# Causal masks from TensorE to VectorE, wider transposes, and a picking matrix made later, in an attention and mixture-of-experts block

## What is computed

```python
h = layernorm(x) * (1 + ca) + sa
q, k, v = (split_heads(h @ W + b) for W, b in ...)     # 16 heads of width 8
att = softmax(where(causal, q @ k.T / sqrt(8), -inf))
y = (att @ v) @ Wo + bo
x = x + ga * (layernorm(y) * gamma + beta)
h = layernorm(x) * (1 + cb) + sb
x = x + gb * (shared_ffn(h) + sum over the top 2 of 8 experts of coef * expert_ffn(h))
```

## Time and profile before

| | |
|---|---|
| runs | 516.39, 521.52, 522.48 us; median 521.52 us |
| span of the profiled execution | 517.1 us, 9099 instructions; the page gives no time of its own beside the span |
| TensorE busy | 468.1 us (91%), 3122 matmuls |
| VectorE busy | 374.1 us (72%), 1046 instructions |
| ScalarE busy | 272.8 us (53%) |
| GpSimd busy | 252.8 us (49%) |
| mean granted TensorE clock | 0.960 |

### The profile page before, as it was taken

The page is one execution under the profiler, slowest core; times in us unless marked ns, Lnnn a source line. Parts: engine busy times, 40 slices in busy tenths (PEclk is TensorE's granted clock), DMA queues, the critical chain, the costliest instruction groups (busy, mean ns, idle before and its releaser), DMA issues. The chain is left out here.

```text
span 517.1 us, 9099 instructions
## 1 busy us (share of the span) xinstructions
PE 468.1 (91%) x3122; PEld 239.6 (46%) x3122; DVE 374.1 (72%) x1046; ACT 272.8 (53%) x571; POOL 252.8 (49%) x344
## 2 busy tenths in 40 slices
PE   3478889999999999999999999999999998899897
PEld 2224334544644553545454453545454454344554
DVE  4687746997589748985699648985789757875165
ACT  2214554775558535765568435764567534755321
POOL 7534356533865077535764077525763251523530
PEclk9857996999999999999999999999999999999999
DMA  4674452332333234323443134323433222003000
GB/s 106 164 171 115 117 152 50 85 94 85 106 99 87 56 113 117 100 69 106 114 101 90 42 111 112 97 61 104 129 83 98 83 77 60 2 2 104 1 21 22
DMA packets 40942, 45.31 MB, mean 88 GB/s; under 512 B 9448, under 2 KB 32520, under 8 KB 40896
## 3 DMA queue, kind: packets, MB, share of 16 engines
q1 hardware_dynamic: 35652, 40.92, 29.9%
q10 hardware_dynamic: 5244, 3.82, 2.6%
HBM read 33.70 MB, written 10.61 MB: 86 GB/s over the span
## 5 line engine op out<-in xcount | busy, mean ns | idle before, releaser
L799 ACT ACTIVATE probs<-s_bank 128x512 f32<-128x512 f32 x320 | 179.9, 596 | 97.2 <-PE s_bank L1199 95.6
L979 DVE CUSTOM_DVE_ANT_0 s_bank<-s_bank,causal_row 128x512 f32<-128x512 f32 (+1 forms) x256 | 156.2, 642 | 28.9 <-PE s_bank L1179 27.3
L1179 PE MATMUL s_bank<-k_stack,q_stack 72*128 72x256 bf16 (+3 forms) x512 | 129.6, 314 | 10.7 <-DVE row_max L979 5.1
L1199 PE MATMUL s_bank<-q_stack,k_stack 75*128 75x128 bf16 (+3 forms) x512 | 120.4, 308 | 15.3 <-DMA q_stack<-max_rows 7.6
L662 POOL TENSOR_SCALAR_AFFINE_SELECT probs<-probs 128x512 f32<-128x512 f32 (+1 forms) x96 | 75.5, 794 | 116.2 <-ACT probs L799 116.0
L1199 PEld LDWEIGHTS s_bank<-q_stack,k_stack 75*128 75x128 bf16 x512 | 43.1, 100 | 92.0 <-ACT probs L799 41.1
L1218 PE MATMUL pv_bank<-probs,v_aug 128*32 128x512 f32 (+3 forms) x1024 | 83.2, 444 | 0.0
L1179 PEld LDWEIGHTS s_bank<-k_stack,q_stack 72*128 72x128 bf16 x512 | 47.3, 100 | 75.0 <-DVE row_max L979 38.5
L984 DVE TENSOR_REDUCE row_max<-s_bank 128x2 f32<-128x512 f32 (+1 forms) x96 | 64.5, 687 | 16.9 <-PE s_bank L1183 16.0
L1218 PEld LDWEIGHTS pv_bank<-probs,v_aug 128*32 128x32 f32 x1024 | 26.1, 110 | 43.8 <-issue 34.2
L1067 DVE SCALAR_TENSOR_TENSOR silu_sb<-tanh_sb,gate_bank 128x512 f32<-128x512 f32 x38 | 26.1, 687 | 21.6 <-ACT tanh_sb L852 21.3
(11 more groups left out here) (183 smaller groups left out, 546.0 us busy)
## 6 DMA issues: line engine op xcount, KB each, us to landing
k_stack<-k_scr SPq DMA_DIRECT2D x96, 96.0 KB
q_stack<-q_scr SPq DMA_DIRECT2D x93, 96.0 KB
coef_all<-coef_scr SPq DMA_DIRECT2D x28, 256.0 KB, 3.9
k_scr<-k_parts SPq DMA_DIRECT2D x32, 96.0 KB, 1.9
q_scr<-q_parts SPq DMA_DIRECT2D x31, 96.0 KB, 1.9
k_scr<-k_parts SPq DMA_DIRECT2D x32, 64.0 KB, 1.8
x_res<-in_L_attn_x SPq DMA_DIRECT2D x8, 256.0 KB, 3.7
x_in<-in_L_attn_x ACTq DMA_DIRECT2D x7, 256.0 KB, 2.8
```

Source lines behind the costliest of these rows:

```text
L799: nc.scalar.activation(dst, src, ACT.Exp, scale=SCALE).then_inc(exp_done, 1)
L979: nc.vector.tensor_tensor_reduce(out=s1_bank[u % 2][:, 0:w], in0=s1_bank[u % 2][:, 0:w], in1=causal_row[:, T - w:T], scale=1.0, scalar=MAS ...
L1179: final = nc.tensor.matmul(dst[:, w * i:w * (i + 1)], q_stack[0:KROWS, h, P * qt:P * (qt + 1)], k_stack[0:KROWS, h, 0:w], start=(i == 0), ...
L1199: final = nc.tensor.matmul(dst[:, at:at + w], k_stack[0:MROWS, hh, P * j:P * (j + 1)], q_stack[0:MROWS, hh, P * j:T], start=True, stop=True)
```

## The change

It does five things.

- VectorE adds all causal masks. The constant `causal` and the matmul of line 1183 are gone, and units 8 to 10 are reduced by one fused add-and-max per head: two instructions with 256 columns for units 8 and 9 each, four with 128 columns for unit 10. `s1_reduced` is counted up by the last of them.
- `row_max` gets five planes instead of three, the last two filled with zeros once, and the transposes of maxima read 80 columns. ScalarE still copies 48 rows.
- `coef` is 72 columns wide per tile instead of 8, the rest zero, and the transposes of coefficients read 72 columns. Later steps take the first 8.
- `pick` and `coef_parts` are no longer made in the head. Four tasks pick0 to pick3 stand in GpSimd's list of turn 0: pick0 fills both with zeros, pick1 to pick3 make one selection each. They have a semaphore of their own, `pick_step`, on which only the tail waits.
- The lists of tasks are written out for every turn (a list "head" with each engine's tasks takes the place of `PROLOGUE`, whose order each engine keeps), and the places of uses of the bank `misc` are counted from TensorE's list. This changes no instruction and no order.

```diff
-        "pool": ("xs xn msplit.0 q k msplit.1 s2.1.3 s2.1.7 s2.1.9 msplit.2 s2.2.3 s2.2.7 s2.2.9 s2.3.3 msplit.3"
+        "pool": ("xs xn msplit.0 q k msplit.1 s2.1.3 s2.1.7 pick0 pick1 s2.1.9 msplit.2 pick2 s2.2.3 pick3 s2.2.7 s2.2.9 s2.3.3 msplit.3"
...
             nc.gpsimd.memset(neg_half[:, :], -0.5)
+            for i in range(2):
+                nc.gpsimd.memset(row_max[i][:, PARTS:MAX_PLANES, :, :], 0.0)
             nc.gpsimd.memset(ident_bf[:, :], 0.0)
-            nc.gpsimd.memset(ones_wide[:, :], 1.0)
-
-            nc.gpsimd.memset(causal[:, :], 0.0).then_inc(const_step, 1)
+            nc.gpsimd.memset(ones_wide[:, :], 1.0).then_inc(const_step, 1)
...
-            final = nc.gpsimd.affine_select(out=causal[:, :], in_=causal[:, :], compare_op=ALU.is_ge, fill=MASKED,
-                                           base=0, pattern=[[-1, P]], channel_multiplier=1)
...
             def late_constants():
                 pool.wait_ge(x_norm, 1)
-                nc.gpsimd.memset(v_aug[1][:, :, :, :], 0.0).then_inc(const_step, 1)
-                nc.gpsimd.memset(pick[:, :, :, :], 0.0)
-                nc.gpsimd.memset(coef_parts[:, :, :], 0.0)
                 nc.gpsimd.memset(bo_parts[:, :], 0.0)
                 nc.gpsimd.memset(ones_bf[:, :], 1.0)
+                nc.gpsimd.memset(coef[:, :, :], 0.0)
+                nc.gpsimd.memset(v_aug[1][:, :, :, :], 0.0).then_inc(const_step, 1)
...
-                for part in range(PARTS):
-                    pool.wait_ge(const_step, 3 + part)
+
+            def tail_constants(part):
+
+                if part == 0:
+                    nc.gpsimd.memset(coef_parts[:, :, :], 0.0)
+                    nc.gpsimd.memset(pick[:, :, :, :], 0.0).then_inc(pick_step, 1)
+                else:
+                    pool.wait_ge(pick_step, part)
                     nc.gpsimd.affine_select(out=pick[:, :, :, :], in_=pick[:, :, :, :], compare_op=ALU.not_equal,
-                                            fill=1.0, base=-part * E, pattern=[[-2, FB], [0, DE], [-1, 2]],
-                                            channel_multiplier=1).then_inc(const_step, 1)
+                                            fill=1.0, base=(1 - part) * E, pattern=[[-2, FB], [0, DE], [-1, 2]],
+                                            channel_multiplier=1).then_inc(pick_step, 1)
...
-                    dve.wait_ge(const_step, 3 + PARTS)
+                    dve.wait_ge(const_step, 3)
...
                     w = P * (qt + 1)
-                    if masked_by_max(a):
-                        if u == 0 and it == 0:
-                            dve.wait_ge(row_masked, 1)
-                        nc.vector.tensor_tensor_reduce(
-                            out=s1_bank[u % 2][:, 0:w], in0=s1_bank[u % 2][:, 0:w], in1=causal_row[:, T - w:T], scale=1.0,
+                    if u == 0 and it == 0:
+                        dve.wait_ge(row_masked, 1)
+                    for i in range(nh):
+                        scores = s1_bank[u % 2][:, w * i:w * (i + 1)]
+                        final = nc.vector.tensor_tensor_reduce(
+                            out=scores, in0=scores, in1=causal_row[:, T - w:T], scale=1.0,
                             scalar=MASKED, op0=ALU.add, op1=ALU.max,
-                            accum_out=row_max[s % 2][:, 0, h, qt].unsqueeze(1)).then_inc(s1_reduced, 1)
-                    else:
-                        nc.vector.reduce_max(row_max[s % 2][:, 0, h:h + nh, qt],
-                                             s1_bank[u % 2][:, 0:nh * w].rearrange("p (h k) -> p h k", h=nh),
-                                             AX_X).then_inc(s1_reduced, 1)
+                            accum_out=row_max[s % 2][:, 0, h + i, qt].unsqueeze(1))
+                    final.then_inc(s1_reduced, 1)
...
-                                                 k_stack[0:KROWS, h, 0:w], start=(i == 0), stop=masked_by_max(a))
-                    if not masked_by_max(a):
-                        diagonal = dst[:, 0:nh * w].rearrange("p (h k) -> p h k", h=nh)[:, :, w - P:w]
-                        final = nc.tensor.matmul(diagonal, ident_bf[:, :], causal[:, :].unsqueeze(1).to_broadcast([P, nh, P]),
-                                                 start=False, stop=True)
+                                                 k_stack[0:KROWS, h, 0:w], start=(i == 0), stop=(i == nh - 1))
...
-                    nc.tensor.transpose(misc_bf[0:PARTS * GH * TT, 0:P],
+                    nc.tensor.transpose(misc_bf[0:MAX_PLANES * GH * TT, 0:P],
...
-                        final = nc.tensor.transpose(misc[0:E, P * t:P * (t + 1)], coef[:, t, :], ident[:, :])
+                        final = nc.tensor.transpose(misc[0:COEF_WIDE, P * t:P * (t + 1)], coef[:, t, :], ident[:, :])
```

More of the change, by code:

```diff
@@ L80 @@
 ORDER = {
+    "head": {
+        "pe": "cond xt k q v gates",
+        "dve": "xs cond xn cols k q gates",
+        "act": "xt k q stack v gates",
+        "pool": "xs late",
+        "sp": "stack",
+    },
     "first": {
@@ L168, in task, with turn_task @@
     return (int(parts[1]), parts[0], int(parts[2]) if len(parts) > 2 else 0)
[L171 to L182, removed]
+def turn_task(it, word):
+    if word[0] == "-":
+        return (it - 1, *task(word[1:]))
+    if word[0] == "+":
+        return (it + 1, *task(word[1:]))
+    return (it, *task(word))
+TURNS = [("head", -1), ("first", 0), *(("middle", b) for b in range(1, B - 1)), ("final", B - 1), ("tail", B)]
+ENGINES = ("pe", "dve", "act", "pool", "sp")
+PROGRAM = {e: [turn_task(it, word) for plan, it in TURNS for word in ORDER[plan][e].split()] for e in ENGINES}
 FILL_TAIL = {("y", 0): 2, ("x2t", 0): 9, ("g", 0): 2}
 MISC_TASKS = ("o", "ot", "x2t", "lg", "ct", "xt", "q", "k", "v", "max")
[L190 to L196, removed]
+MISC_RANK = {x: n for n, x in enumerate(
+    x for x in PROGRAM["pe"] if x[2] in MISC_TASKS and (x[0], x[2]) not in ((-1, "k"), (-1, "v")))}
 def misc_at(it, use):
[L201 to L209, removed]
+    return MISC_RANK[(it, *use)]
 def wait_v(eng, b, misc_read, v_read):
@@ L305, in block_kernel @@
         v_aug = [sb(f"v_aug{i}", [P, TT, H, VC]) for i in range(2)]
-        row_max = [sb(f"row_max{i}", [P, PARTS, GH, TT]) for i in range(2)]
+        row_max = [sb(f"row_max{i}", [P, MAX_PLANES, GH, TT]) for i in range(2)]
         max_rows = sb("max_rows", [PARTS * GH * TT, P], BF16)
@@ L555, in has_next @@
             def has_next(it):
-                return not isinstance(it, int) or it < B - 1
-            walk(sp, "sp", run)
+                return it < B - 1
+            walk("sp", run)
             sp.wait_ge(stored, 16 * (B + 1))
@@ L703, in run @@
                     nc.gpsimd.tensor_tensor(cp[2], coef_rest[:, :, :], cp[1], ALU.subtract).then_inc(coef_split, 1)
-            walk(pool, "pool", run)
+            walk("pool", run)
         @block.scalar
@@ L852, in run @@
                     nc.scalar.activation(tanh_sb[:, :], gate_of(it, a)[:, :], ACT.Tanh, scale=0.5).then_inc(tanh_ready, 1)
-            walk(act, "act", run)
+            walk("act", run)
         @block.vector
@@ L1341, in run @@
                         last_mm.then_inc(down_written, 1)
-            walk(pe, "pe", run)
+            walk("pe", run)
 _INS = ["L0_attn_x", "L0_attn_Wq", "L0_attn_bq", "L0_attn_Wk", "L0_attn_bk", "L0_attn_Wv", "L0_attn_bv",
```

63 lines of the change are left out of this document (27 added, 36 removed).

## The result

The changed kernel takes 551.43 us (median of 4 runs, 549.25 to 552.76) against 519.7 us: ratio 1.0614, 95% interval [1.0541, 1.0686], slower by 31.7 us. The forecast was 529.8, with a range that ended at 540. The direction was right; the size and the upper bound were not.

What follows compares the result with a forecast made beforehand. TensorE was taken as the bound nearly everywhere, VectorE where group 2 ends. Terms -2.0 + 4.9 + 0.6 + 4.5 + 0.3 = +8.3 on 517.1 gave 525.4; the median's 4.4 above that span made it 529.8 us, range 511 to 540.

Steps and rivals of the forecast that it cites:

- Head, -2.0 us: Head: without GpSimd's three selections, VectorE's k_parts gets 1.75 us shorter and q_parts 0.35; -2.0 us in all.
- Turn 0, +4.9 us: First turn: pick tasks delay GpSimd's selects, so TensorE stalls 2.9 us before pv.2.3 and 2.0 before pv.2.0.
- Narrow units, 0.39 and 0.26 us: VectorE: a fused add-and-max takes 0.39 us for 256 columns, 0.26 for 128; eight add 0.8 us per group.
- the rival that priced them dearer: Rival: narrow fused units cost more, felt at group 2's end; 536 us half-way, 542 at worst; chance 0.18 including the clock.
- The two faster rivals: TensorE decides everywhere: 505 us, chance 0.14 (whole or most); GpSimd's added work hidden: 521 to 525, 0.18 (or part gains).
- Ends of groups, +4.5 + 0.6 + 0.3 us: VectorE's extra work at group ends: +4.5 us over six middle turns, +0.6 in the first turn, +0.3 in the last.
- the 57.7 that was named as the sign: Middle turns: a period of 57.7 us, against 57.0 before, would show the forecast right; under 56.9 would show it wrong.
- Transposes: TensorE: 80-column transposes save 0.6 us a turn, 5.0 in all, nearly all lost in waits for VectorE.
- The sum, +8.3 us: Whole kernel: all terms together add 8.3 us to the profiled span of 517.1, giving 525.4.
- The walk through the middle turns: Four group ends of a middle turn in time order: s2.3.0 0.74 us later after group 2, turn 0.75 us longer.

Runs made afterwards that it cites:

- b_rows128: Changed kernel with matmuls over 125 and 128 rows instead of 72 and 75, the added rows adding nothing to the sums: 518.1 us, ratio 0.9996.
- d_steady_masks: Kernel before with 125- and 128-row matmuls, picking matrix in GpSimd's free places of turn 0, 80-column transposes of maxima and all masks on VectorE: 510.97 us.
- c_base: Kernel before with matmuls over 125 and 128 rows and nothing else changed: 508.4 us, ratio 0.984.
- a_masks_back: Changed kernel with units 8 to 10 masked by TensorE and reduced by one instruction each again: 528.9 us, ratio 1.021.
- b_fill_wait: Changed kernel with six matmuls of no use in each middle turn, where TensorE waits at the end of group 2: 531.82 us, ratio 1.019.

## Why the prediction was wrong, point by point

- **Head, -2.0 us: right.** 2.24 in the trace, 1.7 at the end of a run with a steady clock. k_parts at 0.69 bears out that GpSimd's selections had held it up.
- **Turn 0, +4.9 us: right in place and in the stalls, too small in all.** Both stalls stand at the named matmuls, and where the clock is high ahead of the first they last 2.75 and 2.18 us. Moving the four tasks is worth 518.1 - 511.0 = 7.1 us (b_rows128 against d_steady_masks, which ran on different chips and differ in the width of the coefficients' transposes as well); part of it is the lower clock behind the stalls, 13.7 us at 1.2 GHz from 52 us on against 3.4 up to the end of turn 0.
- **Narrow units, 0.39 and 0.26 us: right** (0.38 and 0.25). So VectorE's units cost what was forecast, and the rival that priced them dearer is out as it was worded. The two faster rivals are out too: at a steady clock the masks on VectorE cost 5.0 us more, not 14 less, and GpSimd's added work shows as two stalls.
- **Ends of groups, +4.5 + 0.6 + 0.3 us: right at a steady clock.** 5.0 measured by d_steady_masks; middle period 57.55 in b_rows128 against the 57.7 that was named as the sign. There s2.3.0 comes 228.12 - 212.90 = 15.22 us after s1.2.0, 0.69 later than before (forecast 0.74).
- **Transposes: right.** The switch is gone in the rows, and nearly all of its gain was lost in waits for VectorE, as forecast (0.8 us is left).
- **The sum, +8.3 us: near the mark at a steady clock** (9.7, or 7.9 by the ratios), wrong for the kernel as it runs. Some of the nearness is luck: between the traces of b_rows128 and c_base, turn 0 costs more than forecast and the middle turns less.

The step that failed is the clock, in the prediction's words: "TensorE's granted clock can add to it: from 28 to 57.5 us, where TensorE waits much, its mean was 0.72, so part of the stretch ran at 1.2 GHz, and two new stalls may bring more of that." It looked for the clock where it was already low, in turn 0, and gave it no price of its own. The walk through the middle turns took the 1.00 of the earlier trace rows as given, for the very stretch that it made 0.7 us worse. In its place the runs showed that the clock falls at the end of group 2 in all six middle turns (for 3.4 to 13.7 us). A stretch of 10.24 us costs 3.8 us, some six times what VectorE's delay, which brings it about, costs by itself. A warning stood in the trace, though not among the rows read: one stretch of 0.50 at 283.59 us in the kernel before, near that place. In a_masks_back, with the masks on TensorE, such stretches of 3.41 us stand 1.7 and 1.8 us behind s2.3.0 of turns 3 and 6 (233.30 and 407.38 us). So the place was at the edge before the change.

Where the time went, in us, from the starts of s2.3.0 in the profiled executions:

| stage | before | changed | b_fill_wait | b_rows128 | c_base |
|---|---|---|---|---|---|
| start to s2.3.0 of turn 1 | 111.0 | 120.8 | 120.9 | 113.0 | 104.4 |
| five periods, to s2.3.0 of turn 6 | 286.5 | 305.6 | 290.1 | 287.9 | 285.4 |
| from there to the end | 119.7 | 122.3 | 120.9 | 117.0 | 116.9 |

The change adds 9.8, 19.1 and 2.6 us, where the forecast's terms gave about 4.2 (-2.0 + 4.9 + 0.6 and one middle turn's 0.75), 3.8 (five of them) and 0.3. So the middle turns hold most of the miss. The rest of it is low clock as well: against b_rows128, the low clock costs the changed kernel 17.7 us in the five periods, but also 7.8 ahead of them and 5.3 behind.

## What to carry to other kernels

A short stretch of low clock in one turn of many is no accident to be averaged away: here it marked the place where TensorE worked at the edge, and an edit that adds some tenths of a microsecond of waiting there must be priced with the whole stretch behind it at 1.2 GHz. Look for it with narrow stretches, not with the mean (0.960 here) or the digits of the page. Where such a wait can't be removed, matmuls of no use put into the wait, or matmuls over more of the rows, can cost less than the clock does.
